# First batch shared by two engines, late statistics earlier, last projection bank by bank, first load and last store in halves

## The reference, cut to what matters

```
x = layernorm(x + attn(x))          # attn: norm, qk/v/gate projections with silu, rope, grouped + linear attention, Wo, norm
shared = gelu(x @ Wfc_s + bfc_s) @ Wproj_s + bproj_s
routed = sum over the two chosen of eight experts: gate_e * (gelu(x @ Wfc[e] + bfc[e]) @ Wproj[e] + bproj[e])
out = layernorm(x + shared + routed)
```

## Time and profile before

| what | us |
|---|---|
| median of three runs | 973.26 (972.98 to 974.77) |
| the profiled execution | 973.68 |
| its span in the trace | 971.9 |
| PE busy | 926.9 (95%) |
| DVE busy | 744.6 (77%) |
| ACT busy | 576.6 (59%) |
| POOL busy | 235.2 (24%) |
| before the first product | 11.3 |
| after the last product | 11.1 |

### The profile page before, as it was taken

One profiled execution on the slowest core, in us unless ns is written; L12 is line 12 of the kernel. 1 busy time (PEld: TensorE's weight loads), 2 busy tenths in 40 slices (PEclk: granted clock), 3 DMA queues, 4 the chain that ended last, 5 costly groups with the idle time before them and its releaser, 6 DMA issues.

```text
span 971.9 us, 17985 instructions
## 1 busy us (share of the span) xinstructions
PE 926.9 (95%) x5998; PEld 822.8 (85%) x5998; DVE 744.6 (77%) x1798; ACT 576.6 (59%) x1033; POOL 235.2 (24%) x170
## 2 busy tenths in 40 slices
PE   4979999999999999999999999999999999999994
PEld 3767888788778788899999999999999999999894
DVE  5698898889878599667777777777767899984746
ACT  5525557556645646465555555555555788874754
POOL 0050000000000000414444444444444445520000
PEclk9979999999999999999999999999999999999998
DMA  4130333323225422335555555555555688867302
GB/s 159 50 130 28 108 95 101 102 70 108 71 93 195 151 55 84 103 131 150 140 136 135 137 139 136 140 137 141 150 152 135 183 235 225 231 196 228 109 23 87
DMA packets 66868, 125.88 MB, mean 130 GB/s; under 512 B 13628, under 2 KB 52383, under 8 KB 60288
## 3 DMA queue, kind: packets, MB, share of 16 engines
q1 hardware_dynamic: 48144, 101.02, 31.4%
q0 software_dynamic: 14976, 20.54, 13.0%
q10 hardware_dynamic: 3696, 3.67, 1.1%
HBM read 92.40 MB, written 31.75 MB: 128 GB/s over the span
## 4 chain that ended last, share of the span: by engine, by line
PE 58%; DVE 5%; ACT 2%; issue 1%; DMA 1%; POOL 0%; ACTq 0%; DVEq 0%; POOLq 0%
PE bank L1493 28%; PE bank L1536 27%; PE bank L1521 2%; DVE s_hl L1415 1%; DVE s_acc L1295 1%; DVE s_until_map L1297 1%; DMA s_xb<-x_rows,s_token 1%; DVE s_until_map L1296 1%; ACT s_hh L1165 0%; ACT s_h L1161 0%; ACT s_acc L1182 0%; POOL s_xb L1084 0%; PE bank L1490 0%; DVE s_acc L1377 0%; DVE s_mst L1393 0%
## 5 line engine op out<-in xcount | busy, mean ns | idle before, releaser
L1161 ACT ACTIVATE s_h<-bank,k_bfc 128x512 f32<-128x512 f32 (+1 forms) x248 | 154.4, 623 | 207.6 <-PE bank L1536 194.4
L1415 DVE TENSOR_TENSOR s_hl<-s_h,s_hh 128x512 fp32r<-128x512 f32 (+1 forms) x248 | 151.9, 613 | 133.8 <-ACT s_hh L1165 127.0
L1093 POOL DMA_INDIRECT residual_sums<-s_y,s_dest x78 | 133.3, 1709 | 220.8 <-DVE s_y L1367 204.3
L1084 POOL DMA_INDIRECT s_xb<-x_rows,s_token x78 | 85.3, 1093 | 366.2 <-DVE s_dest L1309 321.0
L1165 ACT ACTIVATE s_hh<-s_h 128x512 fp32r<-128x512 f32 (+1 forms) x248 | 141.4, 570 | 10.7
L1536 PE MATMUL bank<-k_uh,k_wfc1h 128*128 128x512 f32 (+1 forms) x448 | 138.3, 358 | 0.8 <-PEq L191 0.8
L1493 PE MATMUL bank<-s_wpj0l,s_hh 128*128 128x256 f32 x448 | 126.0, 281 | 1.6 <-DVE s_hl L1415 1.6
L1493 PE MATMUL bank<-s_wpj0h,s_hh 128*128 128x256 f32 x448 | 125.8, 281 | 0.0
L1493 PE MATMUL bank<-s_wpj0h,s_hl 128*128 128x256 f32 x448 | 125.6, 280 | 0.0
L1493 PE MATMUL bank<-k_wpj1l,s_hh 128*128 128x256 f32 x400 | 113.0, 282 | 0.4 <-DVE s_hl L1415 0.4
L1493 PE MATMUL bank<-k_wpj1h,s_hl 128*128 128x256 f32 x400 | 112.6, 281 | 0.0
(11 more groups left out here) (297 smaller groups left out, 2150.1 us busy)
## 6 DMA issues: line engine op xcount, KB each, us to landing
k_wstage<-wall SPq DMA_DIRECT2D x50, 1024.0 KB
s_x_in<-x SPq DMA_DIRECT2D x8, 512.0 KB, 4.2
s_x_res<-x SPq DMA_DIRECT2D x8, 512.0 KB, 4.9
x_rows<-s_x SPq DMA_DIRECT2D x8, 512.0 KB, 3.6
residual_sums<-s_x SPq DMA_DIRECT2D x8, 512.0 KB, 4.4
x_parts<-s_x1h SPq DMA_DIRECT2D x8, 512.0 KB, 2.7
x_parts<-s_x1l SPq DMA_DIRECT2D x8, 512.0 KB, 3.7
k_uh<-x_parts SPq DMA_DIRECT2D x8, 512.0 KB, 4.9
```

The lines of the kernel that those rows point to most:

```text
L1084: pool.indirect_dma_start(xb[i][:, t, :], None, X1D, bass.IndirectOffsetOnAxis(token[:, at:at + 1].bitcast(U32), 0), bounds_check=N - 1).t ...
L1093: pool.indirect_dma_start(RES, bass.IndirectOffsetOnAxis(dest[:, at:at + 1].bitcast(U32), 0), y[:, t, :], None, bounds_check=N + S - 1, co ...
L1161: nc.scalar.activation(h[j % 2][:, cols], b[:, cols], ACT.Gelu_apprx_tanh, bias=bfc[w][:, j:j + 1]).then_inc(h_ev, 1)
L1415: tt(hl[j % RING][:, cols], h[j % 2][:, cols], hh[j % RING][:, cols].bitcast(F32), ALU.subtract).then_inc(hl_rd, 1)
```

## The change

Six edits, in three places of the program.

At the start, the load of batch 0 becomes two transfers of two tiles each, and the statistics wait for each half. ACT normalizes tiles 0 and 1, DVE tiles 2 and 3. ACT evacuates and rounds chunk 0, DVE chunk 1, and DVE's subtractions follow. Counts on `xT_ev` and `ld_x` are one lower from there on.

```diff
-            sp.dma_start(x_in[:, :, :], bidx(x_view, 0)).then_inc(ld_x, 16)
+            for h in range(2):
+                half = slice(h * TT // 2, (h + 1) * TT // 2)
+                sp.dma_start(x_in[:, half, :], bidx(x_view, 0)[:, half, :]).then_inc(ld_x0[h], 16)
...
             sp.wait_ge(xn_ready, 1)
+            sp.wait_ge(xn_rest, TT // 2)
...
-            normed(xn, x_in, 0, xn_ready)
+            normed(xn, x_in, 0, xn_ready, range(TT // 2))
             act.wait_ge(ld_v0, 32)
-            x_transposed(0)
+            x_transposed(0, (0,))
...
-            dve.wait_ge(ld_x, 16)
-            stats([x_in[:, t, :] for t in range(TT)], 0)
+            stats([x_in[:, t, :] for t in range(TT)], 0, lambda t: t % 2 or dve.wait_ge(ld_x0[t // 2], 16))
             rstd(0, TT)
             shifts(0, TT)
+            for t in range(TT // 2, TT):
+                norm(xn[:, t, :], x_in[:, t, :], t).then_inc(xn_rest, 1)
...
             weights_lo(0)
-            xT_rest(0)
+            dve.wait_ge(ld_v0, 32)
+            dve.wait_ge(xT_mm, 2)
+            nc.vector.tensor_scalar(xT[:, 1, :], bank[0][:, :], vec[:, L1W + 1:L1W + 2], vec[:, L1B + 1:L1B + 2],
+                                    ALU.mult, ALU.add).then_inc(first_xT, 1)
+            dve.wait_ge(first_xT, 1)
+            dve.wait_ge(xTh_rd, 1)
+            nc.vector.tensor_copy(xTh[:, 1, :], xT[:, 1, :]).then_inc(xTh_rd, 1)
+            dve.wait_ge(xTh_rd, 2)
+            for c in range(KD):
+                tt(xTl[:, c, :], xT[:, c, :], xTh[:, c, :].bitcast(F32), ALU.subtract).then_inc(xTl_rd, 1)
...
             pe.wait_ge(xn_ready, 1)
+            pe.wait_ge(xn_rest, TT // 2)
```

```diff
-        AFTER = [(1, 0), (1, 2), (1, 3), (1, 5), (1, 6), (1, 7), (2, 2), (3, 2), (3, 3), (3, 4), (3, 5)]
+        AFTER = [(1, 0), (1, 2), (1, 3), (1, 5), (1, 6), (1, 7), (2, 2), (2, 3), (2, 4), (3, 2), (3, 3)]
...
-        NORMS = {(LATE[0] + n, j): b for b, (n, j) in enumerate([(1, 5), (1, 6), (2, 1), (2, 3), (3, 5), (3, 6), (3, 7)])}
+        NORMS = {(LATE[0] + n, j): b for b, (n, j) in enumerate([(1, 5), (1, 7), (2, 1), (2, 3), (2, 5), (2, 7), (3, 4)])}
```

```diff
-            for j in (KH - 2, KH - 1):
-                project(LATE[-1], LATE[-1] % 2, j, None, False)
+            n, i, w = LATE[-1], LATE[-1] % 2, side(ROUTED)
+            pe.wait_ge(hl_rd, n * KH + KH - 1)
+            for j, t in ((6, 0), (6, 1), (7, 0), (7, 1), (6, 2), (6, 3), (7, 2), (7, 3)):
+                if (j, t) == (KH - 1, 0):
+                    pe.wait_ge(hl_rd, n * KH + KH)
+                cols = slice(t * P, (t + 1) * P)
+                for hs, ws, last_of in ((hh, 1, False), (hl, 0, False), (hh, 0, j == KH - 1)):
+                    last = mm(yb[i][t // 2][:, t % 2 * D:t % 2 * D + D], hs[j % RING][:, cols], wpj[w][ws][:, j, :], start=False,
+                              stop=last_of, skip_group_check=True)
+                if j == KH - 1 and t % 2:
+                    last.then_inc(last_mm, 1)
...
-            shared_result(LATE[-1], LATE[-1] % 2)
-            for piece in PIECES[len(SUMS):]:
-                total(*piece)
+            dve.wait_ge(ld_y[B - 1], 16)
+            at = (B - 1) * TT
+
+            def statistics_of(t):
+                dve.wait_ge(acc_rd, at + t + 1)
+                return nc.vector.bn_stats(st[:, (B - 1) % 2 * TT + t, :], acc[:, at + t, :])
+
+            for t in range(ST):
+                dve.wait_ge(last_mm, t // 2 + 1)
+                shared_y = yb[LATE[-1] % 2][t // 2][:, t % 2 * D:t % 2 * D + D]
+                tt(acc[:, at + t, :], shared_y, acc[:, at + t, :], ALU.add).then_inc(acc_rd, 1)
+                if t:
+                    statistics_of(t - 1)
+            link(statistics_of(ST - 1))
+            total(*PIECES[-1])
...
-            sp.wait_ge(last_rd, TT)
-            sp.dma_start(out_view[B - 1], acc[:, (B - 1) * TT:, :]).then_inc(o_out, 16)
-            sp.wait_ge(o_out, 16 * B)
+            for h in range(2):
+                half = slice(h * TT // 2, (h + 1) * TT // 2)
+                sp.wait_ge(last_rd, half.stop)
+                sp.dma_start(out_view[B - 1][:, half, :], acc[:, (B - 1) * TT:, :][:, half, :]).then_inc(o_out, 16)
+            sp.wait_ge(o_out, 16 * (B + 1))
```

More of the change, by code:

```diff
@@ L246, in attention @@
         ld_x, ld_r = sem("x_loaded"), sem("residual_loaded")
+        ld_x0, xn_rest, first_xT = [sem(f"first_x_loaded{h}") for h in range(2)], sem("first_xn_rest_ready"), sem("first_xT_evacuated")
         ld_s = sem("shared_weights_loaded")
@@ L381, in weights_hi, with x_transposed @@
                 copy(weights[n][0][:], raws[n]).then_inc(wh_rd, 1)
-            def x_transposed(b):
-                for c in range(KD):
+            def x_transposed(b, chunks=range(KD)):
+                for c in chunks:
                     act.wait_ge(xT_mm, 2 * b + c + 1)
@@ L388, in x_transposed, with normed @@
                                          bias=vec[:, L1B + c:L1B + c + 1]).then_inc(xT_ev, 1)
-                for c in range(KD):
-                    act.wait_ge(xT_ev, 2 * b + c + 1)
+                for c in chunks:
+                    act.wait_ge(xT_ev, 1 if is_int(b) and b == 0 else 2 * b + c)
                     copy(xTh[:, c, :], xT[:, c, :]).then_inc(xTh_rd, 1)
-            def normed(o, i, k, done):
-                for t in range(TT):
+            def normed(o, i, k, done, tiles=range(TT)):
+                for t in tiles:
                     last = nc.scalar.activation(o[:, t, :], i[:, t, :], ACT.Identity, scale=rs[:, k + t:k + t + 1],
@@ L548, in step @@
                 if ahead:
-                    dve.wait_ge(ld_x, 16 * (b + 2))
+                    dve.wait_ge(ld_x, 16 * (b + 1))
                     stats([x_in[:, t, :] for t in range(TT)], 0)
@@ L851, in step @@
                     if ahead:
-                        pe.wait_ge(xT_ev, 2 * (b + 1) + 1)
+                        pe.wait_ge(xT_ev, 2 * (b + 1))
                     if at(B):
@@ L951, in experts @@
         tot_rd, o_rd, o_out = sem("totals_ready"), sem("out_ready"), sem("out_stored")
-        last_rd = sem("last_row_ready")
+        last_rd, last_mm = sem("last_row_ready"), sem("last_products")
         block = ctx.enter_context(nc.Block())
@@ L989, in experts @@
                   ("statistics", (7,)), ("rstd", (7,))]
-        AFTER = [(1, 0), (1, 2), (1, 3), (1, 5), (1, 6), (1, 7), (2, 2), (3, 2), (3, 3), (3, 4), (3, 5)]
+        AFTER = [(1, 0), (1, 2), (1, 3), (1, 5), (1, 6), (1, 7), (2, 2), (2, 3), (2, 4), (3, 2), (3, 3)]
         SUMS = {(LATE[0] + n, j): piece for (n, j), piece in zip(AFTER, PIECES)}
-        NORMS = {(LATE[0] + n, j): b for b, (n, j) in enumerate([(1, 5), (1, 6), (2, 1), (2, 3), (3, 5), (3, 6), (3, 7)])}
-        assert len(LATE) == 4 and FIRST == 4
+        NORMS = {(LATE[0] + n, j): b for b, (n, j) in enumerate([(1, 5), (1, 7), (2, 1), (2, 3), (2, 5), (2, 7), (3, 4)])}
+        assert len(LATE) == 4 and FIRST == 4 and len(SUMS) == len(PIECES) - 2
         HOT = 2 * NT // KH
```

## The result

| what | before | after |
|---|---|---|
| median, five runs each, same chip | 973.66 (972.98 to 976.15) | 969.07 (966.61 to 969.39) |
| the profiled execution | 973.68 | 967.13 |
| its span | 971.9 | 965.2 |
| PE busy | 926.9 | 925.5 |
| last product to the end of the span | 11.0 | 9.25 |

The ratio of the times on record is 0.9935, with an interval from 0.992 to 0.995; of 973.66 that is 4.9 to 7.8 us. The two medians lie 4.59 us apart, just under the lower end. The predicted time was 968.8.

A forecast was written before the change was run, and what follows sets the result against it. PE, busy 95% of the span, was taken as the bound, so only its waits could be won. 1.35 + 0.45 - 0.2 + 1.4 + 1.1 + 0.4 = 4.5 us off 973.26 gave 968.8, range 966.7 to 971.0.

The forecast's parts named there:

- load and statistics: At the start, loading batch 0 in halves lets its statistics end earlier: gain 0.35 us, bounds 0.23 to 0.70.
- normalization: At the start, ACT and DVE normalize two tiles each instead of ACT all four: gain 1.0 us.
- evacuation: At the start, sharing the evacuation between ACT and DVE gains 0; by the cheaper bound 0.26 us.
- start of late round 2: With batch 1 normalized behind chunk 7, PE's projection of chunk 0 no longer waits: gain 0.45 us at most.
- stall at chunk 6 of late round 2: The new place of batches 4 and 5 makes PE wait there: loss 0.2 us, bounds 0 and 0.5.
- end of round 3: PE's 1.41 us wait for chunk 7 shrinks to 0.2: gain 1.4 us, bounds 1.0 and 1.6.
- DVE's sums and statistics: At the end, two sums and one statistic run beside PE's last products: gain 1.1 us, bounds 0.7 and 1.15.
- halves of the store: At the end, storing in two 256 KB halves gains 0.4 us, from none to 0.7.
- the worst bound: For the load at the start: the second half needs the whole 3.64 us again, gain only 0.23 us.
- The clock as a rival: At the start, the clock rises at the same time as before, losing 0.6 us: 969.4 us, chance 0.22.
- The wrong-signs I had named: Qk product later than 15.2, PE gaps over 0.5 us in late round 2 or 3, or a longer middle.
- The middle no longer than before: From 45 to 900 us the kernel should not lengthen; no term of the prediction allowed it.

The follow-up runs named there:

- all_again: The changed kernel unaltered, measured and profiled again beside the kernel before: 968.5 us, ratio 0.9933.
- load_whole: The changed kernel with batch 0 loaded in one transfer instead of two halves: 969.61 us, ratio 0.995.
- start_only: The kernel before with only the start edits (half loads, shared normalization, shared evacuation): 971.97 us, ratio 0.9964.
- round_act: The changed kernel with chunk 1 of batch 0 still evacuated by DVE but rounded by ACT: 968.95 us, ratio 0.9936.
- late_only: The kernel before with only the two tables of the late rounds changed: 973.11 us, ratio 0.9981.
- end_only: The kernel before with only the end edits (last projection and sums bank by bank, store in halves): 974.49 us, ratio 0.9995.
- evac_act: The changed kernel with both chunks of batch 0 evacuated and rounded by ACT again: 969.28 us, ratio 0.9942.
- tail_order: The changed kernel with the last eight projection steps reordered, six instead of four ahead of the first needing chunk 7: 969.3 us, ratio 0.9941.
- store_whole: The changed kernel with batch 7 stored in one transfer instead of two halves: 969.65 us, ratio 0.9949.
- pieces_in_row: The changed kernel with POOL's four long weight operations cut in quarters, all sixteen in a row without spreading: 967.97 us, ratio 0.9936.
- pool_pieces: The changed kernel with POOL's four long weight operations cut in quarters and spread over four attention steps: 959.56 us, ratio 0.9843.
- together: The changed kernel with POOL's quarters spread over four attention steps, chunk 1 rounded by ACT, and the last projection steps reordered: 960.58 us, ratio 0.9853.

## Why the prediction was right, point by point

The forecast was 968.8; the medians are 969.07 and, in all_again, 968.5. That the time was met this closely is in part luck. The forecast took 4.5 from 973.26, the median of three executions of before; with more executions before had medians of 973.66, 974.9, 974.45, 974.88 and 974.12, and 974.9 less 4.5 is 970.4. The gain itself was forecast low: 4.6 us by the first medians, 6.4 by those of all_again and the before beside it, 4.9 to 7.8 by the ratio on record. The terms below hold at their places; what they leave out lies in the middle of the kernel, and is taken up with the clock.

| step of the prediction | said | measured |
|---|---|---|
| load and statistics | 0.35 (0.23 to 0.70) | 0.70, of it 0.57 by the halves (load_whole) and 0.13 by a load that landed earlier anyway |
| normalization | 1.0 | 1.02 |
| evacuation | 0 | -0.06 to -0.08 |
| start of late round 2 | 0.45 | 0.48, in three traces; but 0.37 in start_only, without the table |
| stall at chunk 6 of late round 2 | -0.2 (-0.5 to 0) | -0.37 |
| end of round 3 | 1.4 (1.0 to 1.6) | 1.39 |
| DVE's sums and statistics | 1.1 | 1.12 |
| halves of the store | 0.4 (0 to 0.7) | 0.66 |
| sum | 4.5 | 4.94 |

**The load was mis-sized.** I took the value near the worst bound, since transfers of 128 and 512 KB from SBUF differ by 0.7 only the earlier trace rows. The first half landed at 3.60, 0.77 before the whole did, and the second must have been there 0.71 later, since the four statistics ran through in 1.48. What failed is the assumption behind the worst bound, that a half needs as long as the whole; the measured gain is the upper bound of the prediction.

**The evacuation was right for the sum, not for its term.** I priced DVE's evacuation at 0.68 by a row with the same width; it took 0.81. The other links were shorter than priced, so that only 0.06 of the excess of 0.13 is left. That DVE's own copy is what eats the gain was in the prediction's working, and round_act showed it.

**The stall at chunk 6.** The count of the copy's end was right: in the kernel after, chunk 4's rounded copy ends at 922.26, which with the lead of 3.39 is 925.65, and I had said 925.6. The chain behind it took 8.81 (to 931.07) where I had counted 8.7, and PE wanted its result at 930.87. What I left out are the 0.06 that PE takes to see it and the 0.1 of the first product behind a wait. My own two times were 0.10 apart; 0.10 + 0.11 + 0.06 + 0.1 = 0.37.

**The store was mis-sized.** I interpolated between a landing of 2.2 for 128 KB and 2.9 for 512 KB and got 2.43 for 256. The row of the transfers in the kernel after (count, KB each, median us from issue to landing):

```profile
out<-s_acc SPq DMA_DIRECT2D x2, 256.0 KB, 2.2
```

That is as little as for 128 KB, 0.7 less than the whole, and 0.66 in the span. No row of before had that size; the upper bound, 0.7, was the better guess.

**The clock as a rival.** I gave 0.22 to the case that the clock rises at the same time of day as before and eats 0.6. What happened is a third thing. Over 14 profiled executions the rise came between 17.4 and 21.5 us. That of before, 21.5, was the latest of all. The eleven with the new start, whose first qk product comes 1.1 to 2.1 us earlier, have rises from 17.4 to 20.4, those without it (late_only, end_only and before) 20.0, 20.0 and 21.5. By the rule of the Trainium skill, "TensorE: Matmul & The Clock Gate", Part 1, that the prediction weighed, a moment that is not tied to the kernel's start, the lead would differ from run to run; the traces agree, and by more than I gave it: evac_act gained 1.04 there, tail_order lost 0.31. In the profiled execution after it gave 0.62, which with the 1.1 that came between 30 and 917 us, most of it at 401 and around 797 to 822, is the rest of 6.63: 4.94 + 0.62 + 1.1 = 6.66.

I had no term for the middle, and not all that came there is chance. Around 797 to 822 us the lead grows by 0.72 in five traces (after, start_only, evac_act, load_whole, store_whole) and by 0.44 to 0.56 in the six others with the new start, but only by 0.2 to 0.3 in late_only and end_only, which start as before. So some 0.2 to 0.5 us goes with the new start; why is not shown. Against it, five of the eleven lost 0.7 to 1.4 between 765 and 785 us, and none of the three others did. The sum of the places, 4.9, is thus no measure of the whole gain, which the medians put between 4.6 and 6.4.

**The wrong-signs I had named.** No gap over 0.5 in the late rounds; the qk product at 14.38, where I had said 14.7; 9.25 us behind the last product, where I had said 9.6 (the store). "The middle no longer than before" held in the profiled pair and, by 0.1, in all_again (a lead of 2.35 at 30 us and 2.49 at 900), but not in all traces with the new start: round_act lost 0.86 there and tail_order 0.48, by the late weights and the waits at 400 us. As a sign it was too weak to tell right from wrong.

## What to carry to other kernels

Count the product (or any other operation of the bound engine) in both traces and look where the lead changes: a step has a place and a cause, while the time is a sum with chance in it. A split step gains only what its chain doesn't lose elsewhere: the shared normalization gained 1.0, the shared evacuation nothing until the copy of 0.43 behind it was shared too. And before polishing the ends, look for the longest wait: here an idle engine's four long operations held the vector engine up for as long as they ran, and spreading them gained 9.5 us more where the whole change gained 4.6 to 6.4.

## What was not expected of the hardware

- DVE held up by POOL: an instruction on four columns took 0.16 us alone and up to 1.28 while POOL ran operations of up to 1.30 in a row (pieces_in_row). One on 512 columns took up to 4.87 beside one of 4.81.
- The moment of the clock's first rise lay anywhere from 17.4 to 21.5 us. The second fall, at 390 to 402 us, came in 4 of 14 executions behind a wait of 1.9 to 2.4 us, and not in ten others with waits of 1.65 to 2.2. It costs some 1.6 us. What decides stays open.
- Without the long waits at 60 us (pool_pieces, together) the clock stayed full from 18 to 390 us; with them it fell in each of the 12 others.
